# Both units' outputs in one pass of 256 columns, and what moves with it

## What is computed

```python
q = x @ Wq
kv = x @ Wkv
k, v = jnp.split(kv, 2, axis=-1)
...
sim = jnp.einsum('bid,bjd->bij', q, k) * scale
sim = sim + _cope(q, sim, pos_emb)
attn = jax.nn.softmax(sim, axis=-1)
out = jnp.einsum('bij,bjd->bid', attn, v)
...
return out @ Wout + b_out
```

## Time and profile before

| | us |
|---|---|
| median of 3 runs | 2494.19 |
| lowest and highest | 2493.88, 2496.13 |
| profiled execution | 2493.37 |
| its span | 2491.5 |
| busy in it: TensorE | 2340.9 |
| VectorE | 1814.7 |
| ScalarE | 1745.9 |
| GpSimd | 253.6 |

### The profile page before, as it was taken

The page is one execution under the profiler, slowest core; times in us unless marked ns, Lnnn a source line. Parts: engine busy times, 40 slices in busy tenths (PEclk is TensorE's granted clock), DMA queues, the critical chain, the costliest instruction groups (busy, mean ns, idle before and its releaser), DMA issues. The chain is left out here.

```text
span 2491.5 us, 64093 instructions
## 1 busy us (share of the span) xinstructions
PE 2340.9 (94%) x18687; PEld 1674.2 (67%) x18687; DVE 1814.7 (73%) x4542; ACT 1745.9 (70%) x3767; POOL 253.6 (10%) x417
## 2 busy tenths in 40 slices
PE   7999999999999999999999999999999989999997
PEld 5666666666666666666666666666666656777776
DVE  5888887888888888888888888888888812323231
ACT  5777777777777777777777777777777743444442
POOL 0000000000000000000000000000100001111111
PEclk9999999999999999999999999999999989999998
DMA  2010101010101010101010101010101020101000
GB/s 70 23 38 22 37 21 34 22 38 21 35 22 38 21 35 22 38 21 35 22 38 21 35 22 38 21 37 22 30 13 53 12 63 32 38 25 38 25 27 7
DMA packets 108087, 75.47 MB, mean 30 GB/s; under 512 B 26894, under 2 KB 103823, under 8 KB 107984
## 3 DMA queue, kind: packets, MB, share of 16 engines
q1 hardware_dynamic: 107984, 73.88, 10.8%
HBM read 14.26 MB, written 2.10 MB: 7 GB/s over the span
## 5 line engine op out<-in xcount | busy, mean ns | idle before, releaser
L463 ACT ACTIVATE probsT<-rings 128x512 f32<-128x512 f32 x1024 | 556.4, 595 | 334.9 <-PE rings L615 334.9
L796 DVE TENSOR_REDUCE mx<-Sc 128x1 f32<-128x1024 f32 x512 | 626.8, 1224 | 130.2 <-PE Sc L607 115.1
L615 PEld LDWEIGHTS rings<-ident,probs 128*128 128x128 f32 x4096 | 434.3, 141 | 269.0 <-issue 194.2
L615 PE MATMUL rings<-ident,probs 128*128 128x128 f32 x4096 | 572.9, 283 | 22.1 <-ACT probs L484 1.2
L607 PE MATMUL Sc<-qk,q_now 64*128 64x512 f32 x2048 | 529.6, 615 | 46.8 <-ACT probs L484 26.5
L484 ACT ACTIVATE probs<-Sc,nbias 128x1024 f32<-128x1024 f32 x512 | 566.9, 1121 | 8.6 <-DVE nbias L813 8.6
L629 PE MATMUL out<-probsT,V_now 128*64 128x128 f32 x8192 | 530.0, 277 | 0.0
L629 PEld LDWEIGHTS out<-probsT,V_now 128*64 128x64 f32 x8192 | 439.5, 137 | 58.9 <-issue 45.5
L773 DVE COPY_PREDICATED z<-mask,z 128x224 f32<-128x224 int16 (+5 forms) x768 | 390.8, 509 | 107.6 <-DVE cut L763 33.0
L607 PEld LDWEIGHTS Sc<-qk,q_now 64*128 64x128 f32 x2048 | 188.1, 187 | 232.5 <-issue 231.5
L374 POOL TENSOR_TENSOR prod<-cut,z 128x350 f32<-128x350 f32 x128 | 120.2, 939 | 1577.5 <-DVE z L785 1577.5
(11 more groups left out here) (121 smaller groups left out, 2507.1 us busy)
## 6 DMA issues: line engine op xcount, KB each, us to landing
q_now<-qk SPq DMA_DIRECT2D x256, 64.0 KB, 2.0
xv<-xT SPq DMA_DIRECT2D x113, 128.0 KB, 2.2
q_far<-qk SPq DMA_DIRECT2D x256, 32.0 KB, 1.8
V_now<-V SPq DMA_DIRECT2D x16, 512.0 KB, 3.0
at<-attn SPq DMA_DIRECT2D x16, 512.0 KB, 3.2
probs<-in_x_dram SPq DMA_DIRECT2D x4, 512.0 KB, 5.5
wqk<-in_L_attn_Wq_dram SPq DMA_DIRECT2D x32, 64.0 KB, 2.1
xin<-in_x_dram SPq DMA_DIRECT2D x16, 128.0 KB, 2.8
```

Of the source, the lines that this page charges most:

```text
L463: nc.scalar.activation(probsT[:, u, 4 * s:4 * s + 4, :], ring[k % 2][:, :].rearrange("p (t q) -> p t q", q=P), ACT.Copy).then_inc(slot_out, 1)
L615: last = nc.tensor.transpose(ring[k % 2][:, j * P:(j + 1) * P], probs[:, u, (4 * s + j) * P:(4 * s + j + 1) * P], ident[:, :])
L796: nc.vector.tensor_reduce(mx[:, u, half:half + 1], Sc[:, half * HALF:(half + 1) * HALF], AX.X, ALU.max).then_inc(dve_unit, 1)
```

## The change

1. **Outputs in one pass.** `outputs(g)` runs once a pair for both units: per tile of V one matmul of 256 columns, `probsT[:, :, t, :]`, in place of two of 128. It stands in the first half of the body of pair g + 1, behind the transposes of unit 1. The outputs behind the transposes of unit 0 are gone.
2. **Halves and turns once a pair.** `empty_halves` evicts 256 columns at once, in the first half behind the exps. `turns_of` does both turns between the second and the third slot of unit 0's transposes. `scale` of both units stands at the end of ScalarE's body. `invert` takes both row sums at once.
3. **Projections in the second half.** `project` and `project_values` stand behind the transposes of unit 0. Their evictions stand on ScalarE between the two halves of exp of unit 1. Their slots are 8 and 9 in place of 4 and 5, the transposes of unit 0 have 4 to 7 in place of 6 to 9.
4. **SP.** `q_now` is loaded ahead of the wait for the values' slot, `xv` behind it. `k_near` has a wait of its own on `slot_out`, `V_now` waits for the one pass of the pair before.

```diff
 class Slots:
-    def __init__(self, proj=True):
+    def __init__(self):
         self.last = [0, 1, 2, 3]
-        self.qk, self.values = 4, 5
-        at = 6 if proj else 4
-        self.now = [at, at + 1, at + 2, at + 3]
+        self.now = [4, 5, 6, 7]
+        self.qk, self.values = 8, 9
...
                 if near:
+                    wait_apart(sp, slot_out, base - 1, waited)
                     load_near(g // PAIRS + 1)
                 if head:
-                    wait_apart(sp, out_full, g * 2, waited)
+                    wait_apart(sp, out_full, g, waited)
                     load_values(g)
+                wait_apart(sp, bank_full, g * 4 + 4, waited)
+                load_now(g + 1, not odd)
                 if tile:
                     wait_apart(sp, slot_full, base + Slots().values + 1, waited)
                     load_tile(g + 1)
-                wait_apart(sp, bank_full, g * 4 + 4, waited)
-                load_now(g + 1, not odd)
...
-            def empty_halves(g, u):
-                act.wait_ge(out_full, g * 2 + u + 1)
-                nc.scalar.activation(halves[:, u, :], out[:, 0:P], ACT.Copy).then_inc(halves_out, 1)
+            def empty_halves(g):
+                act.wait_ge(out_full, g + 1)
+                nc.scalar.activation(halves[:, :, :], out[:, 0:2 * P].rearrange("p (u q) -> p u q", q=P),
+                                     ACT.Copy).then_inc(halves_out, 1)
...
-            def outputs(g, u, base, slots, empty=True, tiles=range(NT)):
+            def outputs(g, base, slots, empty=True):
...
-                    last = nc.tensor.matmul(out[half:half + C, 0:P], V_now[:, token_tile(t), :], probsT[:, u, t, :],
-                                            start=t < 2, stop=t >= NT - 2)
+                    last = nc.tensor.matmul(out[half:half + C, 0:2 * P], V_now[:, token_tile(t), :],
+                                            probsT[:, :, t, :], start=t < 2, stop=t >= NT - 2)
...
+            def turns_of(g, evicted=True):
+                pe.wait_ge(halves_out, g + 1)
+                if evicted:
+                    wait_apart(pe, scaled, g * 2, waited)
+                for u in range(2):
+                    last = nc.tensor.matmul(turns[:, u * C:(u + 1) * C], halves[:, u, :], fold[:, :],
+                                            start=True, stop=True)
+                last.then_inc(turned, 1)
...
-                nc.vector.reciprocal(rsum[:, u:u + 1], rowsum[:, u:u + 1]).then_inc(rsum_done, 1)
+                nc.vector.reciprocal(rsum[:, :], rowsum[:, :]).then_inc(rsum_done, 1)
```

More of the change, by code:

```diff
@@ L456, in _, with transposed @@
                     steps(1)
-            def transposed(u, base, slots):
-                for s in range(4):
+            def transposed(u, base, slots, sets=range(4)):
+                for s in sets:
                     k = slots[s]
@@ L498, in body @@
                     transposed(1, base, at.last)
[L499 to L504, removed]
+                exp_half(g, 0, 0)
+                exp_half(g, 0, 1)
                 if not first:
-                    empty_halves(g - 1, 1)
+                    empty_halves(g - 1)
                 if far:
@@ L511, in body @@
                 transposed(0, base, at.now)
+                exp_half(g, 1, 0)
+                if proj:
+                    project(g + PAIRS, not odd, base, at.qk, alone=not val)
+                if val:
+                    values(g, base, at.values)
+                exp_half(g, 1, 1)
                 if not first:
+                    scale(g - 1, 0)
                     scale(g - 1, 1)
-                exps(g, 1)
             body(0, False, first=True)
@@ L617, in transposes @@
                 last.then_inc(slot_full, 1)
-            def outputs(g, u, base, slots, empty=True, tiles=range(NT)):
[L621 to L625, removed]
+            def outputs(g, base, slots, empty=True):
+                if empty:
+                    pe.wait_ge(halves_out, g)
+                wait_apart(pe, v_in, g // PAIRS * 16 + 16, waited)
+                for t in range(NT):
                     if t % 4 == 0:
@@ L628, in outputs @@
                     half = t % 2 * C
-                    last = nc.tensor.matmul(out[half:half + C, 0:P], V_now[:, token_tile(t), :], probsT[:, u, t, :],
-                                            start=t < 2, stop=t >= NT - 2)
[L631 to L636, removed]
-                if evicted:
[L638 to L647, removed]
+                    last = nc.tensor.matmul(out[half:half + C, 0:2 * P], V_now[:, token_tile(t), :],
+                                            probsT[:, :, t, :], start=t < 2, stop=t >= NT - 2)
+                last.then_inc(out_full, 1)
+            def turns_of(g, evicted=True):
+                pe.wait_ge(halves_out, g + 1)
+                if evicted:
+                    wait_apart(pe, scaled, g * 2, waited)
[3 more added lines that the diff above has]
+                last.then_inc(turned, 1)
             def body(g, odd, par, late=False, first=False, proj=True, val=True, far=True, far_par=None,
@@ L651, in body @@
                 base = slots_before(g, late)
-                at = Slots(proj)
+                at = Slots()
                 pe.wait_ge(now_in, g * 32 + 32)
@@ L662, in body @@
                 if not first:
[L663 to L671, removed]
+                    for n in range(4):
+                        transposes(1, base, at.last, n)
+                    outputs(g - 1, base, at.last, empty=not second)
                 if far:
@@ L680, in body @@
                     wait_apart(pe, near_out, g * 2 + 6, waited)
-                transposes_and_turn(g - 1, 0, base, at.now, 1, first)
-                outputs(g, 0, base, at.now, empty=not first)
+                for n in range(4):
+                    transposes(0, base, at.now, n)
+                    if n == 1 and not first:
+                        turns_of(g - 1, evicted=not second)
+                if proj:
+                    weights_at = (g // PAIRS) * 64 + 128 if val else H * 64 - 16
+                    project(g + PAIRS, not odd, base, at.qk, weights_at, alone=not val)
+                if val:
+                    project_values(g + PAIRS, base, at.values)
             def head(at, par, start=0, **kw):
@@ L704, in _ @@
             body(G - 1, True, 1, late=True, proj=False, val=False, far=False)
-            base, at = slots_before(G, True), Slots(proj=False)
+            base, at = slots_before(G, True), Slots()
             pe.wait_ge(exp_done, 4 * G)
-            transposes_and_turn(G - 1, 1, base, at.last, 0)
-            outputs(G - 1, 1, base, at.last)
-            turn(G - 1, 1)
+            for n in range(4):
+                transposes(1, base, at.last, n)
+            outputs(G - 1, base, at.last)
+            turns_of(G - 1)
         @block.vector
@@ L843, in body @@
                 if not first:
-                    invert(g - 1, 1, used=not second)
+                    invert(g - 1, used=not second)
                 if chain:
@@ L863, in body @@
                     last_shift(c)
-                invert(g, 0, used=not first)
             dve.wait_ge(ramped, 1)
@@ L886, in _ @@
             add_halves(G - 1, 1)
-            invert(G - 1, 1)
+            invert(G - 1)
 def general_attention(nc, A):
```

35 lines of the change are left out of this document (16 added, 19 removed).

## The result

The changed kernel takes 2548.5 us (median of 4 runs, 2546.8 to 2551.2) against 2494.0 for the kernel before (2493.5 to 2496.1): ratio 1.022, 95% interval 1.020 to 1.024, 2% slower. The forecast was 2543 with a range of 2496 to 2590, so the sign and the range held. The profiled execution has a span of 2544.8 beside 2491.5 before, +53.3. All times are in us.

The account below looks back on a forecast made before the run. A ring of two legs passing between TensorE and ScalarE was taken as the bound: +0.65 and -0.28 make +0.37 a pair (15.76 against 15.39), 41.1 over 111 pairs, +48.9 with the rest; forecast 2543 us, range 2496 to 2590.

Parts of the forecast that it names:

- The outputs in leg B: Output matmuls behind unit 1's transposes: 32 instructions of 256 columns at 0.109 each plus 0.16, 3.64 us in all.
- leg B: First half, start of unit 1's transposes to start of unit 0's, bound by TensorE: from 8.67 to 8.39, 0.28 shorter.
- the wait ahead of the window: TensorE's 0.30 wait for ScalarE's eviction into `V`, before the 0.51 stretch ahead of the first-half logits: forecast to go.
- The evictions in leg A: `qk` and `V` evicted between exp(1)'s halves on ScalarE: 0.69 a pair, plus some 0.10 for `V` coming late.
- S: The start of unit 0's transposes in a pair, from which times in the second half are counted.
- leg A: Second half, start of unit 0's transposes to start of unit 1's, bound by ScalarE: from 6.72 to 7.37, 0.65 longer.
- The second turn: Two turns instead of one between unit 0's second and third transposes: overhang taken as 0.05, ends 0 and 0.20.
- The pairs with only `qk`: Eight pairs that project `qk` but no values: an estimate of 0.1 each, 0.8 in all.
- The late stage: Six late pairs without projections: 14.97 against 14.63, +0.34 each, 2.0; TensorE's clock was expected to hold.
- A wide pass bound by its weight loads: Rival, faster: 256-column outputs cost 1.90 again, leg B 6.65, total about 2410; chance 0.08.
- Leg A hiding the evictions after all: Rival, about even or a little better, also if leg B loses more than 0.28: 2505 to 2493; chance 0.12.
- R3: The worse rival: hand-overs and outputs at high ends, 0.91 a pair, 2603, or TensorE's clock falls in leg A; chance 0.07.

Follow-up runs that it names:

- the move alone: Kernel before with only the projections moved behind unit 0's transposes, ahead of its outputs, evictions between exp(1)'s halves, outputs left narrow: 2446.7 us, ratio 0.980.

## Why the prediction held, point by point

**The outputs in leg B** were forecast at 3.64 and took 3.61. The two passes of 128 columns (3.71) show the ground for it: cost per column. Leg B came out at 8.34 for 8.39, and the wait ahead of the window went, as forecast.

**The evictions in leg A.** Forecast: first projection at S + 2.93, `V` to start about S + 4.6, the second exp 0.34 behind it. Measured: the projection at S + 2.83, `qk` at S + 4.40, `V` at S + 4.84, the exp at S + 5.01. So it is `qk` that is late, by 0.3, and then the rest takes less (`qk` to `V` to exp 0.44 and 0.17 for 0.35 and 0.34): exp to exp 1.99 for 1.88. The sum was right to 0.11 though its parts were not, which is in part luck. In the kernel with the evictions behind the exps that stretch is 1.09 and the pair 14.89, which shows the cause: in the changed kernel the evictions' place alone costs 0.87 a pair, more than twice the whole loss of 0.37.

**The second turn** overhangs by nothing: third slot at S + 1.34 as in the earlier trace rows (822.83 to 824.17). Leg A was forecast at 7.37 and took 7.42.

**The pair** is 15.75 to 15.77, forecast 15.76; one or two in each head, outside the inner loop, are 15.62. That, and the 2.4 gained at the start, are why 110 pairs and the first two came to 36.0 for 41.1. SP's order cost nothing: no wait for `q_now` or `xv` stands in these pairs.

**The pairs with only `qk`** were an estimate of 0.1 each and took 0.26 (2.1 in eight).

**The late stage** is the step that failed. Its ring was right, 14.86 for 14.97. But of the worse rival I wrote that TensorE's clock would hold in the new idle time, since it held at a wait of 1.36 a pair. The wait became 1.87 there, because leg A has no outputs left in it, and at 1.87 the clock did fall. The row showed one wait length, and I read it as an all-clear for a longer one. Late stage and drain cost 13.4 for the 7.0 forecast; with the gap filled and the clock held they cost 6.1, so the clock is all of the excess. In the main stage the projections fill part of the gap, 0.87 is left, and the clock held (840 to 915):

```profile
840.00:915.00 75.00, 68.24 (x458) 42.66 (x456) 62.61 (x153) 59.41 (x126) 7.07 (x10) 1.00 0.08 20
```

**The total** is nearer than its parts, and that is luck: 53.3 in the profiles for 48.9, made of 5.1 less than forecast in the start and the pairs with both projections, and 1.3, 6.4 and 1.8 more in the pairs with only `qk`, in the late stage with the drain, and in the stages behind.

**The rivals.** A wide pass bound by its weight loads is out (3.61 for 32, and two narrow passes as slow). Leg A hiding the evictions after all is out in the changed kernel (0.87 idle), though it is nearly true of the move alone, where the exp waits for `nbias` anyway (a pair of 14.87 to 15.00, and 14.87 with both evictions behind the exps). Of R3 the clock's half came true, in the late stage alone. What the prediction did not look at is that the change is two changes of opposite sign: +1.39 and -0.45 a pair when each is made alone.

## What to carry to other kernels

Ask of each step that leaves a stretch which engine had it covered: sixteen matmuls that cost nothing beside ScalarE's work cost their full columns in the leg that TensorE bounds, and halving the number of weight loads pays next to nothing back where cost follows the columns. Split a change into its parts before judging it; here a gain of 48 was hidden in a net loss of 54, and setting it free with a better place for two evictions gave 3%. A wait that is long satisfied in the usual pair has to be read at the boundary that it is there for, since an engine's queue stands behind it.

## What the runs showed of the hardware that I had not expected

- TensorE's granted clock fell in some pairs when it was left idle 1.87 once in each pair of 15 to 17, and held at 1.36, 0.87 and 0.56. A fall costs 1.3 to 1.5 in the pair in which it happens (16.2 to 16.4 for 14.86, and 3.60 for 2.23 in one set of logits). Unused matmuls in the gap repaid themselves: -53 in all pairs of one kernel, and -7.3 in the late stage and drain of the other.
- Where TensorE's outer loop turns, a pair of heads each, all kernels lose 2 to 5 in one pair (18.3 to 19.7 before, 18.5 to 19.9 with the change). TensorE is idle there with no releaser in the row (3.49 at 407.31 before, 3.15 at 1432.60 with the change). With a wait at that place it was 6 to 7. The clock falls at some of these turns, too: at one of five before and at four of five with the change, where the granted clock is 0.91 between 1170 and 1190. The five turns cost much the same in sum, 16.2 and 16.9.
- Half as many weight loads in the pass of 256 columns saved 0.04 of 3.71.
